# A recommendation network on one core: 32 table rows fetched by ScalarE's queue behind each part, three gathers fewer on GpSimd, logits laid out as 16 rows

## Chip, core and metric

One core of a Trainium2 chip runs the whole program. The metric is the device time of one execution in microseconds (us); lower is better. PE is the matrix engine (TensorE), ACT is ScalarE, DVE is VectorE, POOL is GpSimd and SP is SyncE, which here only issues DMAs.

## What is computed

A batch of 2048 samples, each with 13 dense numbers and 26 table indices, goes through this network (weights as arguments, batch norm over the batch):

```python
x = dense_inputs                                   # (2048, 13)
for W, b, g, be in bot:                            # 13 -> 512 -> 256 -> 64
    x = _bn(jax.nn.relu(x @ W + b), g, be)
embs = tbl[idx] for each of 26 tables              # (2048, 26, 64), tables of 12500 rows of 64 floats
T = concatenate([embs, x[:, None, :]], axis=1)     # (2048, 27, 64)
Z = einsum('bnd,bmd->bnm', T, T)
R = concatenate([x, Z[:, iu, ju]], axis=1)         # 64 + 351 columns
h = R
for W, b, g, be in top:                            # 415 -> 512 -> 256 -> 1
    h = _bn(jax.nn.relu(h @ W + b), g, be)
return sigmoid(h)
```

## The kernel before

Each engine runs a program of its own, written out by hand and tied to the others by semaphores only; there is no scheduler.

First comes the bottom network on the whole batch (to about 85 us). Meanwhile POOL has already begun to fetch table rows. The batch is cut into 16 parts of 128 samples (`PARTS`). A part needs 26 columns of embeddings, which stand as 13 pairs. One POOL gather (`indirect_dma_start`) fetches one of them for 128 partitions: 128 rows of 256 bytes. Embeddings lie in three slots (`emb[:, s]`), part i in slot i mod 3. POOL may begin a part when DVE has written its row numbers into `stage` (`slot_open`), which DVE does for part i+3 after it has copied part i out of its transposes.

Parts 0 to 14 go through a loop of 5 rounds by 3 slots (`LOOPS`, `SLOTS`). For each part:

- PE transposes the embeddings in four groups of pairs (group 3 is pair 12 alone, and waits for `landed[s][3]`), and DVE copies each group into `TT`. ACT has put the dense column `x` into `TT` (the activations from `x_all`).
- PE forms the products of all pairs, `z`, in two halves (banks `z_bank0` and `z_bank1`), then runs seven matmuls that serve nothing but to keep it busy (`keep_clock(7)`).
- ACT and DVE each copy half of `z` to `Zs` (`take_z`; ACT's half is 16 activations). PE waits for both (`z_taken_a`, `z_taken_v`) and then runs layer 0 of the top network for this part, four blocks of 16 matmul instructions.
- ACT applies Relu to each block twice (to `h0_part` and to `hidden0_hi`), DVE takes statistics.

The last part (15) goes through code of its own in halves h = 0 and 1, each with its own landing semaphores. Then follow layers 1 and 2 of the top network, the statistics of the logits, the sigmoid and one store.

SP shares in the fetch. Where POOL would need one gather, SP can issue 128 direct DMAs of one row each: it loads 16 row numbers into registers, then issues 16 DMAs, and so on. Before the change SP does this for one column of each part in slot 2 (five sets of 128), and for two columns of the last part (two sets of 128, in pieces), which land in a tile of their own, `emb_sp`. These 7 x 128 = 896 DMAs take the place of 7 gathers, so POOL issues 16 x 26 - 7 = 409.

ACT's loop body before, cut:

```python
with act.Fori(0, LOOPS) as it:
    for s in range(SLOTS):
        ...  # TT <- x_all, two activations (L693)
        for h in range(2):
            act.wait_ge(z_done, i * 2 + (h + 1))
            take_z(act_copy, z_bank[h], h, (2, 3)).then_inc(z_taken_a, 1)
        ...  # four blocks: L703, L705
```

Of the kernel before, what the change touches and what calls it, by code (L numbers as in the profile page):

```python
# [72 lines left out]
SP_SLOT = SLOTS - 1
SP_PAIR = TP - 1
SP_LAST = 2
SP_SETS = LOOPS + SP_LAST
SP_BATCH = 16
SP_ORDER = (("part", 0, 0, 128),
            ("last", 0, 0, 96),
            ("part", 1, 0, 128),  # L80
            ("last", 0, 96, 128),
            ("part", 2, 0, 128),
            ("last", 1, 0, 64),
            ("part", 3, 0, 128),
            ("last", 1, 64, 128),
            ("part", 4, 0, 128))
# [10 lines left out]
NPARAM = sum(w for _, w in PARAMS.values())  # L97
# [11 lines left out]
def rec_program(nc, idx, sp_idx, table, dense_t, params, identity, bw0, bw1, bw2, tw0x, twx, tw1, out):  # L109
    ctx = ExitStack()  # L110
    with ctx:
# [17 lines left out]
        sp_raw = sb("sp_raw", [SP_SETS, 2, P], I32)  # L129
        sp_neg = sb("sp_neg", [SP_SETS, P])  # L130
        sp_clamped = sb("sp_clamped", [SP_SETS, P])
        sp_rows = sb("sp_rows", [SP_SETS, P], U32)
        emb_sp = sb("emb_sp", [P, SP_LAST, D])
# [36 lines left out]
        tw2_rep = sb("tw2_rep", [P, K1, QUAD])  # L170
# [31 lines left out]
        consts_ready = sem("consts_ready")  # L202
        slot_open = sem("slot_open")
# [5 lines left out]
        landed_sp_part = sem("landed_sp_part")  # L209
        landed_sp_last = [sem("landed_sp_last%d" % k) for k in range(SP_LAST)]  # L210
# [96 lines left out]

        block = ctx.enter_context(nc.Block())


        @block.sync
        def _(sp):

            sp.dma_start(idx_raw[:, FIRST_COLS], idx[:, FIRST_COLS]).then_inc(first_idx_loaded, 16)
            sp.dma_start(idx_raw[:, LATER_COLS], idx[:, LATER_COLS]).then_inc(idx_loaded, 16)
            sp.dma_start(dense_sb[:, :], dense_t).then_inc(bottom_loaded, 16)
            sp.dma_start(sp_raw[:, :, :], sp_idx).then_inc(sp_idx_loaded, 16)
            sp.dma_start(bw0_sb[:, :], bw0).then_inc(bottom_loaded, 16)
# [10 lines left out]
            regs = [sp.alloc_register("sp_row%d" % r) for r in range(SP_BATCH)]  # L329
            sp.wait_ge(sp_rows_ready, 1)  # L330
            for kind, n, p0, p1 in SP_ORDER:
                if kind == "part":
                    sp.wait_ge(slot_open, n * SLOTS + SP_SLOT + 1)
                for at in range(p0, p1, SP_BATCH):
                    row_set = n if kind == "part" else LOOPS + n
                    sp.load(regs, sp_rows[row_set:row_set + 1, at:at + SP_BATCH])
                    for p, reg in enumerate(regs, at):
                        row = sp.snap(reg, min_val=0, max_val=NF * VOCAB - 1)
                        if kind == "part":
                            sp.dma_start(emb[p:p + 1, SP_SLOT, SP_PAIR, 0, :],  # L340
                                         table[bass.ds(row, 1), :]).then_inc(landed_sp_part, 16)
                        else:
                            sp.dma_start(emb_sp[p:p + 1, n, :],
                                         table[bass.ds(row, 1), :]).then_inc(landed_sp_last[n], 16)
# [49 lines left out]
        def _(pe):  # L394
# [85 lines left out]
            with pe.Fori(0, LOOPS) as it:  # L480
                for s in range(SLOTS):
                    i = it * SLOTS + s

                    for g in range(GROUPS):
                        pairs = group_pairs(g)
                        by_sp = 1 if s == SP_SLOT and SP_PAIR in pairs else 0
                        pe.wait_ge(landed[s][g], (it + 1) * ((len(pairs) * 2 - by_sp) * 16))
                        if by_sp:
                            pe.wait_ge(landed_sp_part, (it + 1) * (P * 16))
# [36 lines left out]
            def last_transposes(h, g):  # L526
# [3 lines left out]
                by_sp = SP_LAST if (h, g) == (0, 0) else 0  # L530
                pe.wait_ge(landed_last[h][g], (k1 - k0 - by_sp) * 16)
                for k in range(by_sp):
                    pe.wait_ge(landed_sp_last[k], P * 16)
# [75 lines left out]
            for k in range(K1):  # L609
                for j in range(CHUNKS):  # L610
                    mm = nc.tensor.matmul(out_bank[0][QUAD * j:QUAD * (j + 1), :], tw2_rep[:, k, :],  # L611
                                          hidden1[:, k, j * CHUNK:(j + 1) * CHUNK],
                                          start=(k == 0), stop=(k == K1 - 1))
                    if (k, j) == (0, CHUNKS - 1):

                        pe.wait_ge(scaled_v["top", 1], 2)
                        pe.wait_ge(bias_ready["top", 0], 1)
                        for kb in range(K1):
                            fold = nc.tensor.matmul(small[:, 8:9], ones[:, :], shift_w2[:, kb:kb + 1],
                                                    start=(kb == 0), stop=(kb == K1 - 1))  # L620
                        fold.then_inc(fold_done["top", 1], 1)
# [12 lines left out]
        def _(act):  # L634
# [52 lines left out]
            with act.Fori(0, LOOPS) as it:  # L687
                for s in range(SLOTS):
                    i = it * SLOTS + s

                    for h in range(2):
                        half = slice(h * D, (h + 1) * D)
                        last = nc.scalar.activation(TT[half, 0, :, NF:V].rearrange("p b v -> p (b v)"),  # L693
                                                    x_all[half, bass.ds(i * (2 * UNIT) + h * UNIT, UNIT)],
                                                    ACT.Copy)
                    last.then_inc(tt_x_written, 1)
# [3 lines left out]
                    for o in range(K0):  # L700
# [6 lines left out]
                                             bias=p_col("top", "b", 0)[:, o:o + 1]).then_inc(l0_relu, 1)  # L707

# [38 lines left out]
            nc.scalar.activation(logits[:, :], out_bank[0], ACT.Relu, bias=bias2["top"][:, :],  # L747
# [14 lines left out]
        def _(dve):  # L762
# [119 lines left out]
            nc.vector.memset(mean_of[:, :], 1.0 / (QUAD * B)).then_inc(consts_ready, 1)  # L882
# [191 lines left out]
```

## Time and profile before

| | |
|---|---|
| median of 3 runs | 573.51 us (572.97 to 573.55) |
| the profiled execution | 573.65 us, span 571.8 us |
| mean granted PE clock | 0.763 of full |
| busy PE / DVE / ACT / POOL | 66% / 42% / 33% / 68% |

The span runs from the first to the last instruction; the 1.85 us between the span and the execution's time lie around it. "Busy" counts an engine's own instructions; issuing a DMA from SP or ACT is not counted, so an engine can be occupied with nothing shown as busy. In the rows, SPq and ACTq are the sequencers of those engines.

### The profile page before, as it was taken

Reading aid. Unit: us, or ns where it says so; the run is one execution under the profiler, and the core shown is the slowest. Engines: PE = TensorE matmul, PEld = TensorE weight load, DVE = VectorE, ACT = ScalarE, POOL = GpSimd, SP = SyncE. Lnnn points to the kernel's source line nnn. Section 1 sums busy time; section 2 is a strip of 40 time slices with the busy share of each in tenths; the row PEclk is TensorE's granted clock in tenths of the full one; section 3 lists DMA queues with packets and bytes.
Section 4 is the critical chain, followed back from the end, with each engine's and each line's share of the span. In section 5 each row is a group of like instructions: output and inputs, shape, how many; then the busy total and the mean of one; then the engine's idle time right before and its main releaser. Section 6 shows DMA issues by size and latency. Waiting matters only on the chain.

```text
span 571.8 us, 16640 instructions
## 1 busy us (share of the span) xinstructions
PE 374.6 (66%) x5806; PEld 281.1 (49%) x5827; DVE 238.8 (42%) x650; ACT 189.5 (33%) x509; POOL 388.8 (68%) x419
## 2 busy tenths in 40 slices
PE   5959768678687572755729181754738182777995
PEld 2328536566565462543517171553526172566682
DVE  5773354644445342424323242423324242455522
ACT  4752144434244141323214041322314041464223
POOL 5777777777777777777777777777777777770100
PEclk9999886896786877585857666585858567598999
DMA  8322122222212221222122121222212121220000
GB/s 240 62 29 28 28 27 31 30 26 31 30 29 30 27 31 29 31 27 30 27 28 30 28 31 26 30 27 29 31 29 29 26 30 26 30 28 7 2 0 2
DMA packets 17500, 18.49 MB, mean 32 GB/s; under 512 B 9302, under 2 KB 10589, under 8 KB 17278
## 3 DMA queue, kind: packets, MB, share of 16 engines
q0 software_dynamic: 13088, 13.43, 17.6%
q1 hardware_dynamic: 4330, 3.96, 2.3%
q8 instruction: 54, 0.88, 0.7%
q14 instruction: 28, 0.22, 0.1%
HBM read 17.35 MB, written 0.01 MB: 30 GB/s over the span
## 4 chain that ended last, share of the span: by engine, by line
POOL 55%; issue 19%; PE 18%; DVE 2%; ACT 2%; DMA 1%; SPq 0%; POOLq 0%; DVEq 0%; ACTq 0%
POOL emb L367 52%; PE l_bank L442 6%; PE l_bank L458 5%; POOL emb L380 3%; PE l_bank L448 3%; PE l_bank L472 2%; PE l_bank L564 1%; DMA emb<-table,stage 1%; ACT Zs L306 1%; PE z_bank L400 1%; DMA par<-params 1%; DVE TT L916 0%; PE l_bank L611 0%; PE l_bank L561 0%; PE tr_bank L536 0%
## 5 line engine op out<-in xcount | busy, mean ns | idle before, releaser
L367 POOL DMA_INDIRECT emb<-table,stage x385 | 363.9, 945 | 120.3 <-issue 117.1
L306 ACT ACTIVATE Zs<-z_bank 27x112 f32<-27x112 f32 (+3 forms) x272 | 92.1, 339 | 200.8 <-PE z_bank L507 179.5
L493 PE MATMUL tr_bank<-ident,emb 128*128 128x128 f32 x195 | 39.1, 330 | 125.8 <-DMA emb<-table,stage 105.5
L280 DVE COPY Zs<-z_bank 27x112 f32<-27x112 f32 (+3 forms) x272 | 88.6, 326 | 51.1 <-PE z_bank L507 43.6
L521 PE MATMUL l_bank<-Zs,tw_sb 128*128 128x128 f32 x840 | 107.2, 281 | 0.0
L521 PEld LDWEIGHTS l_bank<-Zs,tw_sb 128*128 128x128 f32 x840 | 103.1, 199 | 0.0
L916 DVE COPY TT<-tr_bank 128x512 f32<-128x512 f32 (+1 forms) x60 | 54.6, 975 | 97.3 <-PE tr_bank L493 96.8
L493 PEld LDWEIGHTS tr_bank<-ident,emb 128*128 128x128 f32 x195 | 25.9, 163 | 137.5 <-issue 104.0
L507 PE MATMUL z_bank<-TT 64*27 64x26 f32 x3840 | 63.5, 219 | 31.8 <-issue 18.4
L507 PEld LDWEIGHTS z_bank<-TT 64*27 64x27 f32 x3840 | 55.4, 134 | 42.1 <-issue 38.1
L927 DVE BATCH_NORM_STATS2 stats_t<-h_part 128x128 f32 x60 | 17.7, 294 | 112.7 <-ACT hidden_hi L705 110.1
L703 ACT ACTIVATE h_part<-l_bank,par 128x128 f32<-128x128 f32 x60 | 22.1, 368 | 93.2 <-PE l_bank L521 90.0
L400 PE MATMUL tr_bank<-idle_operand 128*128 128x512 bf16 x95 | 42.6, 614 | 5.7 <-issue 5.7
L458 PE MATMUL l_bank<-hidden,bw_sb 13*128 13x512 f32 x32 | 27.7, 1061 | 6.1 <-DMA par<-params 6.1
L442 PE MATMUL l_bank<-hidden_hi,w_hi 128*128 128x512 f32 x64 | 26.4, 413 | 6.7 <-DVE w_hi L824 6.7
L518 PE MATMUL l_bank<-x_all,twx_sb 128*128 x120 | 27.5, 314 | 4.3 <-ACT Zs L306 3.9
L518 PEld LDWEIGHTS l_bank<-x_all,twx_sb 128*128 128x128 f32 x120 | 20.1, 211 | 16.9 <-issue 16.9
L380 POOL DMA_INDIRECT emb<-table,stage x24 | 22.6, 943 | 7.3 <-issue 7.3
L442 PE MATMUL l_bank<-hidden_lo,w_hi 128*128 128x512 f32 x64 | 26.0, 406 | 0.0
L400 PEld LDWEIGHTS tr_bank<-idle_operand 128*128 128x128 bf16 x112 | 13.6, 136 | 22.8 <-issue 21.3
L705 ACT ACTIVATE hidden_hi<-l_bank,par 128x128 f32 x60 | 21.6, 360 | 0.0
L458 PEld LDWEIGHTS l_bank<-hidden,bw_sb 13*128 13x128 f32 x32 | 10.5, 330 | 21.7 <-issue 15.1
(130 smaller groups left out, 279.2 us busy)
## 6 DMA issues: line engine op xcount, KB each, us to landing
emb<-table SPq DMA_DIRECT2D x640, 0.2 KB
emb<-table,stage POOLq DMA_INDIRECT x409, 2.8
emb_sp<-table SPq DMA_DIRECT2D x256, 0.2 KB
tw_sb<-tw0x SPq DMA_DIRECT2D x1, 1792.0 KB
bw_sb<-bw SPq DMA_DIRECT2D x1, 512.0 KB, 3.8
tw_sb<-tw SPq DMA_DIRECT2D x1, 512.0 KB
twx_sb<-twx SPq DMA_DIRECT2D x1, 256.0 KB
idx_raw<-idx SPq DMA_DIRECT2D x1, 169.0 KB, 2.5
```

Of the source, the lines that this page charges most:

```text
L280: last = copy(dst, src[:, :, ZC * q:ZC * q + w])
L306: return nc.scalar.activation(dst, src, ACT.Copy)
L367: pool.indirect_dma_start(out=emb[:, s, k, h, :], out_offset=None, in_=table, in_offset=bass.IndirectOffsetOnAxis(ap=stage[:, s, col:col + ...
L380: pool.indirect_dma_start(out=emb_last[:, h, k, :], out_offset=None, in_=table, in_offset=bass.IndirectOffsetOnAxis(ap=stage[:, LAST_SLOT, ...
L400: nc.tensor.matmul(bank[:, :], idle_operand[:, 0:P], idle_operand[:, :], start=True, stop=True)
L442: nc.tensor.matmul(bank, w1_scaled["hi"][:, k, o * P:(o + 1) * P], hidden0[part][:, k, ch * CHUNK:(ch + 1) * CHUNK], start=(n == 0 and par ...
L458: nc.tensor.matmul(bank, bw0_sb[:, o * P:(o + 1) * P], dense_sb[:, ch * CHUNK:(ch + 1) * CHUNK], start=True, stop=True).then_inc(mm_done[" ...
L493: tr = nc.tensor.transpose(tr_bank[g % 2][:, c * P:(c + 1) * P], emb[:, s, k, :, :].rearrange("p h d -> p (h d)"), ident[:, :])
L507: mm = nc.tensor.matmul(bank[QUAD * j:QUAD * j + V, x * ZM:(x + 1) * ZM], one, one[:, 1:V], start=True, stop=True)
L518: nc.tensor.matmul(acc, twx_sb[:, cols], x_all[:, bass.ds(i * (2 * UNIT), 2 * UNIT)], start=True, stop=False)
L521: mm = nc.tensor.matmul(acc, tw0_sb[:, c, cols], Zs[:, c, :], start=False, stop=(c == ZC - 1))
L916: nc.vector.tensor_copy(TT[:, 0, :, n0:n0 + w].rearrange("p b n -> p n b"), tr_bank[g % 2][:, 0:w * UNIT].rearrange("p (n b) -> p n b", n= ...
```

## The change

ACT's loop over the parts is written out instead of looping. Behind each of the parts 1 to 12 ACT issues 32 direct row DMAs (two loads of 16 row numbers, then 16 DMAs each). The column of slot 2 is still fetched whole by SP. A column of slot 1 is now fetched in rows too: for part 1 by SP alone, for parts 4, 7, 10 and 13 rows 0 to 31 by SP and 96 rows by ACT, a third behind each of the three parts ahead of it. The two columns of the last part go back to POOL. So rows take the place of 10 gathers, and POOL issues 16 x 26 - 10 = 406. `write_x(i + 1)`, ACT's copy of the dense column for the next part, now stands before the row DMAs. The logits are computed as a bank of 128 columns with 16 rows in use, instead of 512 columns with 4, by 32 narrow matmuls in place of 8 wide ones.

```diff
+LB = CHUNK // P
+LROW = QUAD // LB
...
-SP_ORDER = (("part", 0, 0, 128),
...
+ROW_SLOTS = (1, 2)
+ROW_BATCH = 16
+SP_ROWS = 32
+ACT_ROWS = P - SP_ROWS
+SP_ORDER = ((1, 0, P), (2, 0, P), (1, 1, SP_ROWS), (2, 1, P), (1, 2, SP_ROWS), (2, 2, P),
+            (1, 3, SP_ROWS), (2, 3, P), (1, 4, SP_ROWS), (2, 4, P))
...
+        def fetch_rows(engine, regs, slot, n, p0, p1):
+
+            row_set = ROW_SLOTS.index(slot) * LOOPS + n
+            for at in range(p0, p1, ROW_BATCH):
+                engine.load(regs, sp_rows[row_set:row_set + 1, at:at + ROW_BATCH])
+                for p, reg in enumerate(regs, at):
+                    row = engine.snap(reg, min_val=0, max_val=NF * VOCAB - 1)
+                    engine.dma_start(emb[p:p + 1, slot, ROW_PAIR, 0, :],
+                                     table[bass.ds(row, 1), :]).then_inc(landed_rows[slot], 16)
...
+            for slot, n, p1 in SP_ORDER:
+                sp.wait_ge(slot_open, n * SLOTS + slot + 1)
+                fetch_rows(sp, sp_regs, slot, n, 0, p1)
...
-                            if (s, k, h) == (SP_SLOT, SP_PAIR, 0):
+                            if s in ROW_SLOTS and (k, h) == (ROW_PAIR, 0):
                                 continue
...
-                        if h == 0 and k < SP_LAST:
-                            continue
...
+                        by_row = 1 if s in ROW_SLOTS and ROW_PAIR in pairs else 0
+                        pe.wait_ge(landed[s][g], (it + 1) * ((len(pairs) * 2 - by_row) * 16))
+                        if by_row:
+                            pe.wait_ge(landed_rows[s], (it + 1) * (P * 16))
...
-            with act.Fori(0, LOOPS) as it:
+            write_x(0)
+            for it in range(LOOPS):
                 for s in range(SLOTS):
...
+                    if i + 1 < LAST:
+                        write_x(i + 1)
+                    if 1 <= i <= LAST - SLOTS:
+                        n, third = divmod(i - 1, SLOTS)
+                        first = SP_ROWS + third * (ACT_ROWS // SLOTS)
+                        act.wait_ge(sp_rows_ready, 1)
+                        act.wait_ge(slot_open, (n + 1) * SLOTS + 2)
+                        fetch_rows(act, act_regs, 1, n + 1, first, first + ACT_ROWS // SLOTS)
...
-            nc.scalar.activation(logits[:, :], out_bank[0], ACT.Relu, bias=bias2["top"][:, :],
+            nc.scalar.activation(logits[:, :], out_bank[0][:, 0:P], ACT.Relu, bias=bias2["top"][:, :],
                                  accum_out=logit_sum[:, :]).then_inc(logit_summed, 1)
...
-                    last = nc.vector.tensor_scalar(tw2_rep[:, k, :], ones[:, 0:QUAD],
+                    last = nc.vector.tensor_scalar(tw2_col[:, k, 0:LB * QUAD:QUAD + LROW], ones[:, 0:LB],
```

Smaller edits that go with it: `tw2_col` is cleared at the start in place of filling `mean_of`, `mean_of` is then made from `ones` and a new column of `params` that is 1/2048 on every eighth partition, and the store writes 16 rows of 512 bytes instead of 4 of 2048.

On ACT, between the last Relu of one part and the first copy of `z` of the next, these instructions stand before the change (ISA and REGISTER_ALU are work on registers):

```order
L703 ACTIVATE h_part<-l_bank,par 128x128 [waits l0_done]
L705 ISA
L705 ACTIVATE hidden_hi<-l_bank,par 128x128
L693 ISA
L693 ACTIVATE TT<-x_all 64x64
L693 ISA
L693 ACTIVATE TT<-x_all 64x64
L698 ISA
L306 ACTIVATE Zs<-z_bank 27x16x7 [waits z_done]
```

After the change, at the same place between part 1 and part 2 (the middle of the 32 DMAs cut):

```order
L699 ACTIVATE h_part<-l_bank,par 128x128 [waits l0_done]
L701 ACTIVATE hidden_hi<-l_bank,par 128x128
L683 ACTIVATE TT<-x_all 64x64 x2
L307 TENSOR_LOAD sp_rows [waits slot_open,sp_rows_ready]
L309 ISA
L310 DMA emb<-table 1x64
...
L307 TENSOR_LOAD sp_rows
L309 ISA
L310 DMA emb<-table 1x64
...
L301 ACTIVATE Zs<-z_bank 27x16x7 [waits z_done]
```

Two loads and 32 pairs of a register instruction and a DMA now stand ahead of the first copy of the next part's `z`.

On POOL, the loop body and the last part before (x25 means 25 alike in a row):

```order
L367 DMA emb<-table,stage 128x64 [waits slot_open]
L367 DMA emb<-table,stage 128x64 x25
L360 REGISTER_ALU
L367 DMA emb<-table,stage 128x64 [waits slot_open]
L367 DMA emb<-table,stage 128x64 x25
L360 REGISTER_ALU
L367 DMA emb<-table,stage 128x64 [waits slot_open]
L367 DMA emb<-table,stage 128x64 x24
...
L380 DMA emb<-table,stage 128x64 [waits slot_open]
L380 DMA emb<-table,stage 128x64 x23
```

and after:

```order
L361 DMA emb<-table,stage 128x64 [waits slot_open]
L361 DMA emb<-table,stage 128x64 x25
L354 REGISTER_ALU
L361 DMA emb<-table,stage 128x64 [waits slot_open]
L361 DMA emb<-table,stage 128x64 x24
L354 REGISTER_ALU
L361 DMA emb<-table,stage 128x64 [waits slot_open]
L361 DMA emb<-table,stage 128x64 x24
...
L372 DMA emb<-table,stage 128x64 [waits slot_open]
L372 DMA emb<-table,stage 128x64 x25
```

Each round of three parts has one gather less, and the last part has two more.

## Rows read from the trace of the kernel before

**Rows 1.** Page: chain that ended last, by engine and line

```profile
POOL 55%; issue 19%; PE 18%; DVE 2%; ACT 2%; DMA 1%; SPq 0%; POOLq 0%; DVEq 0%; ACTq 0%
```

**Rows 2.** Timeline of POOL: start, length, operation, [idle before]; first and last gathers

```profile
4.48 1.13 POOL L367 DMA_INDIRECT emb<-table,stage  x1 [3.21 <-DVE stage L859]
5.92 0.94 POOL L367 DMA_INDIRECT emb<-table,stage  x1 [0.31 <-issue]
...
484.57 0.94 POOL L367 DMA_INDIRECT emb<-table,stage  x1 [0.30 <-issue]
...
508.28 0.94 POOL L380 DMA_INDIRECT emb<-table,stage  x1 [0.30 <-issue]
...
514.52 0.94 POOL L380 DMA_INDIRECT emb<-table,stage  x1 [0.30 <-issue]
```

**Rows 3.** Timeline from part 14 into the last part, all engines

```profile
487.55 0.47 PE L493 MATMUL tr_bank<-ident,emb 128*128 128x128 f32 x1 [0.24 <-DMA emb<-table,stage]
488.89 2.03 PE L507 MATMUL z_bank<-TT 64*27 64x26 f32 x132 [0.87 <-DVE TT L916]
...
491.11 2.88 ACT L306 ACTIVATE Zs<-z_bank 27x112 f32<-27x112 f32 x8 [15.71 <-PE z_bank L507]
...
505.21 0.27 PE L536 MATMUL tr_bank<-ident,emb_sp 128*128 128x128 f32 x1
...
509.69 4.27 ACT L306 ACTIVATE Zs<-z_bank 27x56 f32<-27x56 f32 x16 [1.60 <-PE z_bank L550]
...
512.55 1.11 PE L536 MATMUL tr_bank<-ident,emb 128*128 128x128 f32 x4 [2.07 <-DMA emb<-table,stage]
...
514.45 0.70 PE L561 MATMUL l_bank<-twx_sb,x_all 128*64 128x128 f32 x4
```

**Rows 4.** Timeline of ACT, parts 1 and 2 (start, length)

```profile
109.94 5.90 ACT L306 ACTIVATE Zs<-z_bank 27x112 f32<-27x112 f32 x16 [5.95 <-PE z_bank L507]
118.17 0.37 ACT L703 ACTIVATE h_part<-l_bank,par 128x128 f32<-128x128 f32 x1 [2.33 <-PE l_bank L521]
...
123.80 0.36 ACT L705 ACTIVATE hidden_hi<-l_bank,par 128x128 f32 x1
124.05 0.65 ACT L693 ACTIVATE TT<-x_all 64x64 f32 x2
130.59 2.89 ACT L306 ACTIVATE Zs<-z_bank 27x112 f32<-27x112 f32 x8 [5.89 <-PE z_bank L507]
```

**Rows 5.** Timeline of SP's queue: runs of DMA issues (start, length)

```profile
8.65 63.78 SPq L340 DMA_DIRECT2D emb<-table  x128
73.87 46.90 SPq L343 DMA_DIRECT2D emb_sp<-table  x96
...
194.23 14.76 SPq L343 DMA_DIRECT2D emb_sp<-table  x32
210.42 63.15 SPq L340 DMA_DIRECT2D emb<-table  x128
```

**Rows 6.** Lines of SP's queue: durations in ns min/median/max, first and last start

```profile
L336 SPq TENSOR_LOAD <-sp_rows x56: 1136/1229/1384, 7.2 to 459.8; - x56
L340 SPq DMA_DIRECT2D emb<-table x640: 224/225/567, 8.7 to 467.5; - x160
```

**Rows 7.** Register work on ACT's queue: durations in ns, first and last start

```profile
L705 ACTq FUSED_REGOPS  x45: 46/51/51, 99.3 to 505.4; - x45
```

**Rows 8.** Timeline of PE, layer 0 of parts 2 and 14

```profile
134.96 2.77 PE L400 MATMUL tr_bank<-idle_operand 128*128 128x512 bf16 x6 [0.33 <-issue]
138.04 0.79 PE L518 MATMUL l_bank<-x_all,twx_sb 128*128 x2 [0.31 <-ACT Zs L306]
138.62 2.38 PE L521 MATMUL l_bank<-Zs,tw_sb 128*128 128x128 f32 x14
140.84 0.39 PE L518 MATMUL l_bank<-x_all,twx_sb 128*128 x2
...
476.17 0.66 PE L493 MATMUL tr_bank<-ident,emb 128*128 128x128 f32 x4 [1.54 <-DMA emb<-table,stage]
486.19 1.11 PE L493 MATMUL tr_bank<-ident,emb 128*128 128x128 f32 x4 [9.36 <-DMA emb<-table,stage]
...
499.85 0.39 PE L518 MATMUL l_bank<-x_all,twx_sb 128*128 x2
501.64 0.39 PE L518 MATMUL l_bank<-x_all,twx_sb 128*128 x2
```

**Rows 9.** Windows: stretch, length, busy of PE, PEld, DVE, ACT, POOL, clock, DMA share, GB/s

```profile
467.00:478.00 11.00, 8.29 (x70) 7.81 (x68) 4.25 (x10) 3.03 (x10) 8.46 (x9) 0.97 0.22 26
478.00:498.00 20.00, 8.79 (x269) 5.77 (x271) 6.84 (x20) 5.61 (x16) 15.11 (x17) 0.50 0.20 28
498.00:512.00 14.00, 11.31 (x205) 9.95 (x205) 6.03 (x20) 6.73 (x21) 10.38 (x11) 0.99 0.22 29
```

**Rows 10.** Timeline of the end: logits, their statistics, sigmoid

```profile
563.33 1.06 PE L611 MATMUL l_bank<-hidden,tw_rep 128*32 128x512 f32 x8
564.46 0.69 ACT L747 ACTIVATE logits<-l_bank,bias_top 128x512 f32<-128x512 f32 x1 [4.19 <-PE l_bank L611]
565.97 0.72 ACT L751 ACTIVATE logit_sq<-logits,neg_mean 128x512 f32<-128x512 f32 x1 [0.73 <-DVE neg_mean L1011]
568.85 0.81 ACT L756 ACTIVATE prob<-logits,norm_top 128x512 f32<-128x512 f32 x1
```

More of the change, by code:

```diff
@@ L70 @@
 CHUNKS = B // CHUNK
+LB = CHUNK // P
+LROW = QUAD // LB
 CU = CHUNK // UNIT
 PW = NF
[L73 to L77, printed above, removed]
-SP_ORDER = (("part", 0, 0, 128),
[L79 to L86, printed above, removed]
+ROW_PAIR = TP - 1
+ROW_SLOTS = (1, 2)
+ROW_SETS = len(ROW_SLOTS) * LOOPS
+ROW_BATCH = 16
[3 more added lines that the diff above has]
+            (1, 3, SP_ROWS), (2, 3, P), (1, 4, SP_ROWS), (2, 4, P))
 FIRST_COLS = slice(0, SLOTS * PW)
@@ L96 @@
 PARAMS["top", "W", 2] = (sum(w for _, w in PARAMS.values()), K1)
-NPARAM = sum(w for _, w in PARAMS.values())
+NPARAM = sum(w for _, w in PARAMS.values()) + 1
 def group_pairs(g):
@@ L128, in rec_program @@
         stage = sb("stage", [P, SLOTS, PW], U32)
[L129 to L133, printed above, removed]
+        sp_raw = sb("sp_raw", [ROW_SETS, 2, P], I32)
+        sp_neg = sb("sp_neg", [ROW_SETS, P])
+        sp_clamped = sb("sp_clamped", [ROW_SETS, P])
+        sp_rows = sb("sp_rows", [ROW_SETS, P], U32)
         emb = sb("emb", [P, SLOTS, TP, 2, D])
@@ L174, in rec_program @@
         mean_of = sb("mean_of", [P, P])
-        logits = sb("logits", [P, CHUNK])
+        logits = sb("logits", [P, P])
         logit_sum = sb("logit_sum", [P, 1])
         neg_mean = sb("neg_mean", [P, 1])
-        logit_sq = sb("logit_sq", [P, CHUNK])
+        logit_sq = sb("logit_sq", [P, P])
         sq_sum = sb("sq_sum", [P, 1])
-        prob = sb("prob", [P, CHUNK])
+        prob = sb("prob", [P, P])
         tr_bank = [ps("tr_bank%d" % k, [P, GROUP * P]) for k in range(2)]
@@ L202, in rec_program @@
         consts_ready = sem("consts_ready")
+        mean_of_ready = sem("mean_of_ready")
         slot_open = sem("slot_open")
@@ L208, in rec_program @@
         sp_rows_ready = sem("sp_rows_ready")
-        landed_sp_part = sem("landed_sp_part")
-        landed_sp_last = [sem("landed_sp_last%d" % k) for k in range(SP_LAST)]
+        landed_rows = {s: sem("landed_rows%d" % s) for s in ROW_SLOTS}
         landed_last = [[sem("landed_last%d_%d" % (h, g)) for g in range(len(LAST_GROUPS))] for h in range(2)]
@@ L327, in _ @@
             sp.dma_start(w1_sb["top"][:, :, :], tw1.rearrange("(k p) n -> p k n", p=P)).then_inc(top_loaded, 16)
-            regs = [sp.alloc_register("sp_row%d" % r) for r in range(SP_BATCH)]
+            sp_regs = [sp.alloc_register("sp_row%d" % r) for r in range(ROW_BATCH)]
             sp.wait_ge(sp_rows_ready, 1)
[L331 to L344, printed above, removed]
+            for slot, n, p1 in SP_ORDER:
+                sp.wait_ge(slot_open, n * SLOTS + slot + 1)
+                fetch_rows(sp, sp_regs, slot, n, 0, p1)
             sp.wait_ge(prob_ready, 1)
-            sp.dma_start(out, prob[0:P:QUAD, :]).then_inc(stored, 16)
+            sp.dma_start(out.rearrange("q (j b) -> (q j) b", j=LB), prob[0:P:LROW, :]).then_inc(stored, 16)
             sp.wait_ge(stored, 16)
@@ L485, in _ @@
                         pairs = group_pairs(g)
[L486 to L489, printed above, removed]
+                        by_row = 1 if s in ROW_SLOTS and ROW_PAIR in pairs else 0
+                        pe.wait_ge(landed[s][g], (it + 1) * ((len(pairs) * 2 - by_row) * 16))
+                        if by_row:
+                            pe.wait_ge(landed_rows[s], (it + 1) * (P * 16))
                         if g >= 2:
@@ L529, in last_transposes @@
                 k0, k1 = LAST_GROUPS[g]
[L530 to L533, printed above, removed]
+                pe.wait_ge(landed_last[h][g], (k1 - k0) * 16)
                 for c, (k, k_end) in enumerate(last_blocks(g)):
-                    source = emb_sp if h == 0 and k < SP_LAST else emb_last[:, h, :, :]
                     tr = nc.tensor.transpose(last_tr_bank[g][0:(k_end - k) * D, c * P:(c + 1) * P],
-                                             source[:, k:k_end, :].rearrange("p k d -> p (k d)"),
+                                             emb_last[:, h, k:k_end, :].rearrange("p k d -> p (k d)"),
                                              ident[:, :])
@@ L609, in _ @@
             for k in range(K1):
[L610 to L621, printed above, removed]
+                for j in range(LB):
+                    for q in range(NQ):
+                        first = (q * LB + j) * P
+                        mm = nc.tensor.matmul(out_bank[0][QUAD * q:QUAD * (q + 1), 0:P],
+                                              tw2_col[:, k, j * QUAD:(j + 1) * QUAD], hidden1[:, k, first:first + P],
+                                              start=(k == 0 and j == 0), stop=(k == K1 - 1 and j == LB - 1))
+                if k == 0:
+                    pe.wait_ge(scaled_v["top", 1], 2)
+                    pe.wait_ge(bias_ready["top", 0], 1)
+                    for kb in range(K1):
+                        fold = nc.tensor.matmul(small[:, 8:9], ones[:, :], shift_w2[:, kb:kb + 1],
+                                                start=(kb == 0), stop=(kb == K1 - 1))
+                    fold.then_inc(fold_done["top", 1], 1)
             mm.then_inc(logits_done, 1)
             keep_clock(3, z_bank[0])
+            pe.wait_ge(mean_of_ready, 1)
             pe.wait_ge(logit_summed, 1)
@@ L686, in _, with write_x @@
             act.wait_ge(cleared, 1)
-            with act.Fori(0, LOOPS) as it:
+            act_regs = [act.alloc_register("act_row%d" % r) for r in range(ROW_BATCH)]
+            def write_x(i):
+                for h in range(2):
+                    half = slice(h * D, (h + 1) * D)
+                    last = nc.scalar.activation(TT[half, 0, :, NF:V].rearrange("p b v -> p (b v)"),
+                                                x_all[half, i * (2 * UNIT) + h * UNIT:i * (2 * UNIT) + (h + 1) * UNIT],
+                                                ACT.Copy)
+                last.then_inc(tt_x_written, 1)
+            write_x(0)
+            for it in range(LOOPS):
                 for s in range(SLOTS):
                     i = it * SLOTS + s
[L691 to L696, printed above, removed]
                     for h in range(2):
@@ L881, in _ @@
             nc.vector.memset(eps_col[:, :], EPS).then_inc(consts_ready, 1)
-            nc.vector.memset(mean_of[:, :], 1.0 / (QUAD * B)).then_inc(consts_ready, 1)
+            nc.vector.memset(tw2_col[:, :, :], 0.0).then_inc(consts_ready, 1)
             dve.wait_ge(consts_ready, 5)
             dve.wait_ge(bottom_loaded, 48)
+            nc.vector.tensor_scalar_mul(mean_of[:, :], ones[:, :], par[:, NPARAM - 1:NPARAM]).then_inc(mean_of_ready, 1)
             for n in range(CHUNKS * K0):
@@ L1044 @@
         params[:, at:at + width] = columns(vec)
+    params[0:P:LROW, NPARAM - 1] = 1.0 / B
     w0 = get("L0_rec_top_W0")
@@ L1054 @@
     cols = idx.reshape(UNIT * 2, PARTS, TP, 2)
-    sets = ([(it * SLOTS + SP_SLOT, SP_PAIR) for it in range(LOOPS)] + [(LAST, k) for k in range(SP_LAST)])
+    sets = [(it * SLOTS + s, ROW_PAIR) for s in ROW_SLOTS for it in range(LOOPS)]
     sp_idx = np.stack([np.stack([cols[:, part, k, 0], (2 * k + np.arange(P) // UNIT) * VOCAB]) for part, k in sets])
```

2 lines of the change are left out of this document (1 added, 1 removed).

## The prediction

> **What bounds the kernel now.** I read the chain that ended last first: POOL has 55% of it and "issue" 19%, most of it the pause between POOL's gathers [rows 1]. POOL's timeline shows why: from 5.92 to 484.57 us gathers 2 to 385 start every 1.25 us (478.65 / 383) and POOL never waits for anything, neither for a slot nor for a transfer [rows 2]. So each gather is worth 1.25 us until the last part. There, [rows 3] show that other bounds stand close: part 14's chain gives PE back at 505.2; the last part's copies of `z` end at 509.69 + 4.27 = 513.96; the gather begun at 508.28 [rows 2] lets PE transpose at 512.55; and both meet at the layer 0 that starts at 514.45. The end goes by whichever is later: POOL, or the chain over PE and ACT.
>
> The second view is therefore ACT's timeline. Between parts it looks free: before part 14 it waits 15.71 us for `z` [rows 3]. But in parts 1 and 2 it waits only 5.9 us [rows 4], since PE has only just begun on the parts (the bottom network ran until 85 us) and catches up with POOL: a part takes 130.59 - 109.94 = 20.65 us there, against some 32 in POOL's pace.
>
> **POOL's term.** Three gathers fewer by 1.25 us: -3.75 us, if POOL still sets the end. `slot_open` gives POOL a lead of two whole parts, some 63 us, so a part that is up to that much late doesn't stop it.
>
> **What a fetch costs ACT.** The trace has no DMA issued by ACT. The nearest rows are SP's, which runs the same load, register instruction and DMA in the same order. 32 rows with one load among them took 14.76 us [rows 5], and the load ahead adds about 1.3 (the gap from 72.43 to 73.87), so 16.0 us. From below: were all but the DMAs' own 225 ns and the loads' shortest 1136 ns hidden [rows 6], 32 x 0.225 + 2 x 1.14 = 9.5 us. Nothing at all is excluded, since the DMAs stand in the same queue ahead of the next copy of `z`. From above: with each DMA as long as the longest of SP's, 567 ns instead of 225 [rows 6], 16.0 + 32 x 0.34 = 26.9 us. I take 16.0: register work costs ACT's queue 51 ns [rows 7], small as on SP, and SP's pace is the only measured one for this whole sequence.
>
> The DMA engines aren't the issue: they are busy 0.20 to 0.22 of the time [rows 9], and 384 rows of 256 bytes on ACT are in number what 3 gathers fetch.
>
> **ACT's period with the fetch.** From the first copy of `z` to the end of `TT<-x_all` ACT takes 124.70 - 109.94 = 14.8 us [rows 4]. All of this waits on itself: PE's layer 0 needs ACT's copies, the Relus need layer 0. With 16.0 behind it the period is 30.8 us. That fits into POOL's 31.7 (76 gathers for three parts, 95.0 us) by a hair. But two things don't fit.
>
> First, the last third of the rows for parts 4, 7, 10 and 13 is issued directly ahead of that very part. PE can finish its transposes only when they have landed: from a gather's end at 485.51 to PE's transpose 2.0 us, to `z` 1.4, to ACT's copy 2.2, in sum 5.6 us [rows 2, 3] in which ACT waits. Three parts then take ACT 3 x 30.8 + 5.6 = 98.0 us, more than POOL's 95.0.
>
> Second, the catching up is gone. Before, parts went at 20.65 us until PE reached POOL at about part 5. Now they go at 30.8 from part 1 on and never reach it.
>
> **The chain, step by step.** Copies of `z` of part 1 start at 109.94, as before. SP must issue 256 rows for parts 1 and 2 instead of 128: 73.87 + 63.4 = 137.3 [rows 5], plus 5.6, so part 2's copies start at 142.9 (ACT itself is free at 140.7; before it was 130.59). Part 3: 173.7. Part 4: 173.7 + 30.8 + 5.6 = 210.1. Part 13: 210.1 + 3 x 98.0 = 504.1. Behind it stands no fetch, so part 14 follows at the quick pace: 524.8. Before it was 491.11 [rows 3]. All that follows stands on this: **+33.7 us**, and POOL's 3.75 are hidden below it. The last part's rows have all landed by then; its own chain over copies and layer 0 is as long as before, so 0 here. SP's later sets stay ahead of need: part 5's end at 137.3 + 16.0 + 65 = 218, and PE could use them at about 228.
>
> **PE's clock.** PE now idles ahead of layer 0. In a period of 30.8 us it has the same work of about 20.65, so about 10 us of nothing between the last filler matmul and layer 0, in the seven parts (3, 5, 6, 8, 9, 11, 12) where ACT isn't waiting for rows. In the trace an idle of 9.36 us [rows 8] was followed by a granted clock of 0.50, which is 1.2 GHz, for the 20 us from 478 to 498, after 0.97 ahead of it [rows 9]. A block of layer 0 takes 1.79 us at 2.4 GHz (499.85 to 501.64) and up to twice that at 1.2; part 2's first block, caught on the rise, took 2.80 [rows 8]. I take one block at half clock in each of the seven: 7 x 1.8 = **+12.5 us**. The bounds are 0, and all four blocks slow, 7 x 7.2 = +50. The Trainium skill ("TensorE: Matmul & The Clock Gate", HAM oscillation) says that a wait for data lets the clock drop, so that the next batch starts cold each time; by that rule the term is at least mine. The trace agrees for the waits on gathers, and shows none yet for a wait on ACT.
>
> **Logits.** Three activations shrink from 512 to 128 columns: 0.69, 0.72 and 0.81 us [rows 10] become about 0.37, as the 128-column Relu in [rows 4] does, so -1.1. PE's half on the path, 8 instructions in 1.06 us [rows 10], becomes 32 of a quarter of the width: the same columns, with more instructions, 0 to +0.8; I take +0.3. Together **-0.8**. The multiply for `mean_of` and the larger clear fall where DVE waits for PE in the bottom network; uncovered they would be some 0.5 us. The unrolling takes a few register instructions from ACT, hidden in its waits before.
>
> **Sum.** 573.65 (the profiled execution's own time, 0.14 above the median) + 33.7 + 12.5 - 0.8 = 619.1, forecast **619 us**.
>
> **Rivals.** (1) *ACT issues faster than SP, and the change does what POOL's row promises.* ACT's lateness falls by 12 us for each us by which a fetch is shorter (12 fetches in the chain). To be back at part 14's new due time, 491.1 - 3.75, it must lose 37.4 us, so the fetch must take 12.9 us or less. Then POOL sets the end: 573.65 - 3.75 - 0.8 = 569.1 us, faster. For it: the lower bound 9.5 is inside; ACT's long wait in steady state [rows 3] is as long as one fetch. Against it: 225 ns are only half of SP's measured step of 0.42 us, and I see no reason for the other half to vanish on ACT. The skill's page "Perfetto Trace Analysis" (DMA Optimizations) would have it so: where descriptor generation binds, balancing DMAs over the engines that can issue them may help. By that rule the result would be 569. Its page "DMA: Bandwidth & Descriptors" (Issuing engines are not separate DMA queues) says that this saves only the issuing sequencer's time; no run here shows either yet. Chance 0.18.
>
> (2) *The fetch is as on SP, but the clock stays low through layer 0* (or the fetch is slower by 2 us): 573.65 + 33.7 + 50 - 0.8 = 657 at the full bound; 643 with 18 us a fetch and my clock term. Above 650: chance 0.10.
>
> (3) *The fetch lies between*, 13 us, and the loss cancels the gain within 0.2% (what a measurement of this kernel can just tell from no change, 1.1 us): only a window of 0.2 us in the fetch's length does this. Chance 0.02.
>
> (4) *The forecast*: fetch of 14 to 18 us, some clock loss. From 573.65 + 33.7 - 24 - 0.8 = 583 (14 us, no clock loss) to 619 + 24 = 643 (18 us), with a longer clock loss 650. Chance 0.70; its own range is 583 to 650. Above 0.2% slower in all: 0.80, rival 2 within it. The range over all reaches from rival 1's 568 to 650.
>
> **What the profile after should show.** Runs of 32 row DMAs in ACT's queue of 16 us each (if about 12, rival 1). Gathers still 1.25 us apart, the last starting at about 510.8, with PE going on long after. ACT's first copies of `z` about 31 us apart in two of three parts and 36 in the third, waiting for no one in the two. Part 13's copies near 504 plus the clock's share. PE idle 10 us ahead of layer 0, with the clock at 0.5 there. The forecast is wrong if ACT still waits for `z` in most parts, or if the rows' landing isn't what PE waits for in parts 4, 7, 10 and 13.

## The result and the profile after

The changed kernel takes 602.93 us (median of 4, 601.71 to 603.51) against 573.52 us before: a ratio of 1.0497, with a 95% interval of 1.0471 to 1.0524. It is slower by 29.4 us. The profiled execution took 603.06 us with a span of 601.2 us. Here and below a ratio leaves out executions that lie more than 1.5% above the fastest of their kernel.

The page of the profile of the kernel after, the chain that ended last by engine and by line, answers to [rows 1]:

```profile
PE 46%; ACTq 23%; ACT 15%; issue 10%; DVE 4%; DMA 1%; SPq 0%; DVEq 0%
PE l_bank L513 19%; ACTq L310 16%; ACT Zs L301 12%; PE l_bank L434 5%; PE l_bank L450 5%; PE z_bank L499 4%; ACTq L307 4%; PE l_bank L510 4%; ACTq L309 3%; PE l_bank L440 3%; PE l_bank L464 2%; DVE TT L921 2%; PE l_bank L552 1%; ACT TT L683 1%; DMA emb<-table 1%
```

POOL had 55% of the chain before; now it isn't in it. In its place stands ACT's queue (ACTq) with 23%: L310 issues the row DMAs, L307 loads row numbers, L309 is the register instruction. POOL itself did just what the prediction's term for it says. Its last gather, the 406th, against 514.52 before [rows 2]:

```profile
511.04 1.04 POOL L372 DMA_INDIRECT emb<-table,stage  x1 [0.31 <-issue]
```

It starts 3.5 us sooner, and PE goes on with parts long after. ACT's waits, sums over the span (us in total, times, longest):

```profile
ACT Zs L301 <- issue: 114.5, 8, 14.5
ACT h_part L699 <- PE l_bank L513: 112.0, 60, 4.2
ACT Zs L301 <- PE z_bank L499: 92.9, 11, 19.3
```

In 8 parts ACT comes to its copies of `z` with no wait for PE: the idle time of its datapath, up to 14.5 us each, ends by "issue", which is the queue at work on DMAs. The timeline of ACT shows a period (parts 3, 4 and 5; start, length, engine, operation, idle before):

```profile
173.03 5.66 ACT L301 ACTIVATE Zs<-z_bank 27x112 f32<-27x112 f32 x16 [14.37 <-issue]
...
189.42 0.36 ACT L701 ACTIVATE hidden_hi<-l_bank,par 128x128 fp32r<-128x128 f32 x1
189.67 0.66 ACT L683 ACTIVATE TT<-x_all 64x64 f32<-64x64 f32 x2
190.57 14.00 ACTq L310 DMA_DIRECT2D emb<-table  x32
209.66 2.89 ACT L301 ACTIVATE Zs<-z_bank 27x112 f32<-27x112 f32 x8 [19.33 <-PE z_bank L499]
...
223.70 0.36 ACT L701 ACTIVATE hidden_hi<-l_bank,par 128x128 fp32r<-128x128 f32 x1
223.95 0.66 ACT L683 ACTIVATE TT<-x_all 64x64 f32<-64x64 f32 x2
224.86 14.23 ACTq L310 DMA_DIRECT2D emb<-table  x32
239.14 3.20 ACT L301 ACTIVATE Zs<-z_bank 27x112 f32<-27x112 f32 x9 [14.53 <-issue]
```

The reader is to see two things. From 224.86 to 239.09 the queue issues, and the copies of part 5 start at 239.14, at once. From 190.57 to 204.57 it issues the last third for part 4, and then ACT waits 5.1 us more, until 209.66: rows landing, transpose, `z`. Later copies start at 499.38 (part 13) and 519.86 (part 14), against 459.43 and 491.11 before: part 14 is 28.8 us late, and that is nearly the whole loss of 29.4.

Most of this lateness is there early. Part 4's copies start at 209.66 against 175.78 before, and from part 4 to part 13 ACT takes 96.6 us for each round of three parts (289.72 / 3), only 1.6 us more than POOL's 95.0. Part 14, with no fetch ahead of it, then wins some back.

The queues' rows, durations in ns min/median/max, answer to [rows 6]:

```profile
L310 ACTq DMA_DIRECT2D emb<-table x384: 213/214/524, 129.5 to 494.6; - x192
L307 ACTq TENSOR_LOAD <-sp_rows x24: 1184/1249/1537, 128.1 to 487.3; - x24
```

PE's timeline in part 5, from the end of its filler on, answers to [rows 8]:

```profile
234.00 2.52 PE L392 MATMUL tr_bank<-idle_operand 128*128 128x512 bf16 x6 [0.33 <-issue]
245.05 0.79 PE L510 MATMUL l_bank<-x_all,twx_sb 128*128 x2 [8.53 <-ACT Zs L301]
245.63 3.19 PE L513 MATMUL l_bank<-Zs,tw_sb 128*128 128x128 f32 x14
248.62 0.64 PE L510 MATMUL l_bank<-x_all,twx_sb 128*128 x2
249.05 2.01 PE L513 MATMUL l_bank<-Zs,tw_sb 128*128 128x128 f32 x14
250.89 0.39 PE L510 MATMUL l_bank<-x_all,twx_sb 128*128 x2
```

and the windows over it (the granted clock is the third number from the right):

```profile
239.00:250.00 11.00, 4.95 (x24) 4.96 (x25) 0.36 (x2) 6.10 (x18) 8.30 (x9) 0.53 0.25 29
250.00:262.00 12.00, 7.72 (x123) 6.69 (x121) 5.03 (x12) 2.41 (x8) 9.22 (x10) 1.00 0.20 31
```

After 8.53 us without work the first block of layer 0 takes 3.57 us (245.05 to 248.62), twice the 1.79 of [rows 8], in a window with 0.53 granted (near the lower level, 1.2 GHz); the second takes 2.27, and from 250 on the clock is 1.00 (2.4 GHz). In all seven parts where PE waits for ACT (3, 5, 6, 8, 9, 11, 12) the first block takes 3.57 us, the second 2.12 to 3.05, and the third 1.79.

### The profile page after: what moved, and what is told of

Its sections match the earlier page's. It is cut to its first block, busy times and chain, and to the rows that moved or that the text cites. A ratio compares the mean times of both kernels' runs of the same rounds, so it can differ in the third digit from the quotient of the medians.

```text
span 601.2 us, 17737 instructions
## 1 busy us (share of the span) xinstructions
PE 390.2 (65%) x5853; PEld 300.9 (50%) x5875; DVE 236.4 (39%) x651; ACT 187.4 (31%) x509; POOL 386.3 (64%) x416
## 4 chain that ended last, share of the span: by engine, by line
PE 46%; ACTq 23%; ACT 15%; issue 10%; DVE 4%; DMA 1%; SPq 0%; DVEq 0%
PE l_bank L513 19%; ACTq L310 16%; ACT Zs L301 12%; PE l_bank L434 5%; PE l_bank L450 5%; PE z_bank L499 4%; ACTq L307 4%; PE l_bank L510 4%; ACTq L309 3%; PE l_bank L440 3%; PE l_bank L464 2%; DVE TT L921 2%; PE l_bank L552 1%; ACT TT L683 1%; DMA emb<-table 1%
## 5 line engine op out<-in xcount | busy, mean ns | idle before, releaser
L513 PE MATMUL l_bank<-Zs,tw_sb 128*128 128x128 f32 x840 | 123.7, 308 | 0.0
L513 PEld LDWEIGHTS l_bank<-Zs,tw_sb 128*128 128x128 f32 x840 | 119.8, 226 | 0.0
L485 PE MATMUL tr_bank<-ident,emb 128*128 128x128 f32 x195 | 33.8, 305 | 94.6 <-DMA emb<-table 61.5
L499 PE MATMUL z_bank<-TT 64*27 64x26 f32 x3840 | 66.1, 217 | 30.0 <-issue 14.2
L921 DVE COPY TT<-tr_bank 128x512 f32<-128x512 f32 (+1 forms) x60 | 52.4, 980 | 64.1 <-PE tr_bank L485 63.7
L485 PEld LDWEIGHTS tr_bank<-ident,emb 128*128 128x128 f32 x195 | 23.8, 151 | 103.4 <-issue 71.7
L510 PE MATMUL l_bank<-x_all,twx_sb 128*128 x120 | 30.4, 343 | 51.3 <-ACT Zs L301 51.3
L510 PEld LDWEIGHTS l_bank<-x_all,twx_sb 128*128 128x128 f32 x120 | 22.9, 237 | 63.4 <-issue 63.4
L701 ACT ACTIVATE hidden_hi<-l_bank,par 128x128 fp32r<-128x128 f32 x60 | 21.6, 360 | 0.0
```

Of the source, the lines that this page charges most:

```text
L485: tr = nc.tensor.transpose(tr_bank[g % 2][:, c * P:(c + 1) * P], emb[:, s, k, :, :].rearrange("p h d -> p (h d)"), ident[:, :])
L499: mm = nc.tensor.matmul(bank[QUAD * j:QUAD * j + V, x * ZM:(x + 1) * ZM], one, one[:, 1:V], start=True, stop=True)
L510: nc.tensor.matmul(acc, twx_sb[:, cols], x_all[:, bass.ds(i * (2 * UNIT), 2 * UNIT)], start=True, stop=False)
L513: mm = nc.tensor.matmul(acc, tw0_sb[:, c, cols], Zs[:, c, :], start=False, stop=(c == ZC - 1))
L921: nc.vector.tensor_copy(TT[:, 0, :, n0:n0 + w].rearrange("p b n -> p n b"), tr_bank[g % 2][:, 0:w * UNIT].rearrange("p (n b) -> p n b", n= ...
```

## The experiments

In each, "stretch" is the time from ACT's first copy of a part's `z` to the end of its last Relu. The kernels with 28 and 24 rows, with rows set aside and with more filler ran once each, so their times have no interval; the differences read from their times are 12 us and more, where the executions of the kernel before lie within 5 us (572.88 to 577.59). More filler, at 3 us, is read by its trace.

**ACT issues no rows.** The changed kernel without ACT's fetches; 96 of 128 rows of one column stay unfetched in parts 4, 7, 10 and 13.

```diff
-                    if 1 <= i <= LAST - SLOTS:
...
-                        fetch_rows(act, act_regs, 1, n + 1, first, first + ACT_ROWS // SLOTS)
...
-                            pe.wait_ge(landed_rows[s], (it + 1) * (P * 16))
+                            pe.wait_ge(landed_rows[s], (it + 1) * (P * 16) if s != 1 else P * 16 + it * ((SP_ROWS + 3 * ACT_FETCH) * 16))
```

> The changed kernel, but ACT issues no row DMAs: 96 of the 128 rows of one column in parts 4, 7, 10 and 13 are not fetched, and PE waits for SP's 32 alone. Theory (ACT's fetch sets the pace): PE catches up with POOL again by about part 5, POOL's 406 gathers set the end, 573.65 - 3.75 - 0.8 = about 569 us. Rival (it is SP's 256 rows for parts 1 and 2, or the unrolled ACT program, that cost the time): still above 585.

Measured: 568.24 us (567.42 to 569.04), a ratio to before of 0.9876 (0.9831 to 0.9922). ACT's timeline at part 14:

```profile
485.36 2.87 ACT L302 ACTIVATE Zs<-z_bank 27x112 f32<-27x112 f32 x8 [15.39 <-PE z_bank L500]
```

ACT waits for PE again, and part 14 is 5.8 us ahead of before. SP's rows for part 2 are still late there (its copies start at 141.75 against 130.59), and it costs nothing at the end. The 34.7 us between this kernel and the changed one are ACT's fetches, with the wait for their rows and the clock that they cost, and without them the gathers saved bring the kernel to about the 569.1 us of the prediction's first rival.

**28 and 24 rows in each fetch.** The second load and its DMAs cut short, the rest of the rows not fetched.

```diff
-                        fetch_rows(act, act_regs, 1, n + 1, first, first + ACT_ROWS // SLOTS)
+                        fetch_rows(act, act_regs, 1, n + 1, first, first + ACT_FETCH)
```

> The changed kernel with 28 rows in each of ACT's 12 fetches instead of 32 (4 rows in each third are not fetched). Theory: each fetch is 4 x 0.38 to 0.40 = 1.6 us shorter and all 12 lie on the chain, so 602.9 - 19 = about 584 us. Rival (lateness comes once, from the start, not from each fetch): within 3 us of the changed kernel.

> As the kernel with 28, with 24 rows in each fetch. The chain over ACT would come to 602.9 - 38 = 565 us, below POOL's bound of 569; so 569 to 573 by the theory, bent by the floor and not 38 below. Rival (one-time lateness): no change from 602.

Measured: 585.88 and 568.92 us. From 32 to 28 rows the time falls by 17.1 us, 1.4 for each of 12 fetches; from 28 to 24 by another 17.0, down to about the kernel with no rows on ACT. Part 5's copies stand at 239.14, 232.57 and 227.38 us with 32, 28 and 24, part 13's at 499.38, 479.92 and 458.99. The steps grow from 6.6 and 5.2 us to 19.5 and 20.9, so the lateness comes with each fetch and not once. With 28 rows the fetch behind part 1 isn't on the chain: part 2 waits for SP's rows, until 143.36. And with 24 ACT waits 11.49 us for `z` ahead of part 14, against 6.06 with 28, so by then it has some 5 us to spare and is out of the bound.

One thing more stands in these two traces. A round of three parts, from part 4's copies to part 13's, takes 91.7 us with 28 rows and 86.1 with 24. With 28 ACT is thus quicker than POOL's 95.0, and the kernel is still 12.4 us slower than before: it reaches part 4 late (204.90 against 175.78) and hasn't caught up by part 14.

**Rows set aside.** ACT issues all 384 DMAs, into a tile that nobody reads; PE doesn't wait for them, so 96 rows of the column are old ones.

```diff
+                        engine.dma_start(aside[p:p + 1, aside_at, :],
+                                         table[bass.ds(row, 1), :]).then_inc(landed_aside, 16)
```

> The changed kernel with ACT's 384 rows landing in a tile that no one reads until the end; PE waits for SP's 32 rows alone in parts 4, 7, 10 and 13 (96 rows of that column are not the right ones). It takes away the wait for rows just issued and keeps ACT's queue as it is. Theory: the four waits of 5.1 us go, and PE then idles ahead of layer 0 in those parts too, at some 2 us of slow clock each: 602.9 - 20 + 8 = about 590 us. Rival (landing of the rows is the whole trouble): 569.

Measured: 587.66 us. ACT's waits:

```profile
ACT Zs L304 <- issue: 156.7, 11, 14.4
ACT h_part L706 <- PE l_bank L520: 111.0, 60, 4.1
ACT Zs L304 <- PE z_bank L506: 35.3, 7, 18.6
```

"Issue" now ends the wait in 11 parts instead of 8, and of the 29.4 us lost 14 remain. So the wait for the landing of rows just issued costs about 15 us net, and the occupied queue alone, with no data needed, still puts the kernel above before.

**More filler.** 29 filler matmuls instead of 7 in slots 0 and 2.

```diff
-                    keep_clock(7, tr_bank[0])
+                    keep_clock(7 if s == 1 else 29, tr_bank[0])
```

> The changed kernel with 29 filler matmuls instead of 7 behind z in slots 0 and 2 (parts 0, 2, 3, 5, 6, 8, 9, 11, 12, 14). They fill 5 to 9 us of PE's wait for ACT. Theory (a low clock lengthens layer 0 behind that wait): in parts 3, 5, 6, 8, 9, 11 and 12 the stretch from ACT's first copy to its last Relu falls from 16.0-16.9 to about 14.3 us, 15 us in all, while parts 0 and 14, where ACT doesn't make PE wait, pay up to 5 us each: 588 to 598 us. Rival (the longer stretch has another cause, such as contention with the row DMAs): the stretches stay above 16 us.

Measured: 599.96 us, 2 us above the expected range. PE's timeline in part 5, and in part 8:

```profile
235.48 5.75 PE L392 MATMUL tr_bank<-idle_operand 128*128 128x512 bf16 x24
244.52 0.48 PE L510 MATMUL l_bank<-x_all,twx_sb 128*128 x2 [3.29 <-ACT Zs L301]
244.84 1.73 PE L513 MATMUL l_bank<-Zs,tw_sb 128*128 128x128 f32 x14
246.41 0.39 PE L510 MATMUL l_bank<-x_all,twx_sb 128*128 x2
...
328.71 7.78 PE L392 MATMUL tr_bank<-idle_operand 128*128 128x512 bf16 x28 [0.34 <-issue]
339.35 0.79 PE L510 MATMUL l_bank<-x_all,twx_sb 128*128 x2 [2.87 <-ACT Zs L301]
339.94 3.19 PE L513 MATMUL l_bank<-Zs,tw_sb 128*128 128x128 f32 x14
342.92 0.64 PE L510 MATMUL l_bank<-x_all,twx_sb 128*128 x2
```

In part 5, with 3.29 us idle instead of 8.53, the first block takes 1.89 us. In parts 3, 5 and 9 the stretch fell from 16.1-16.8 to 14.0 us, as expected; in 6, 11 and 12 only to 15.5-15.7, and in part 8 not at all (16.9). Over the seven parts it went from 115.3 to 105.9 us, 9.4 of the 15 I had expected. Part 14 paid: its layer 0 starts 4.6 us after its copies are done.

So the slow blocks hang on what PE does ahead of them: nothing but filler was added, and in three parts they went. But the length of the idle time just ahead of layer 0 doesn't sort the parts. In 3, 5 and 9 it was 1.64, 3.29 and 1.42 us, and the first block took 1.88 or 1.89. In 6, 8, 11 and 12 it was 1.85, 2.87, 2.65 and 2.12 us, no longer than in part 5, and the first block took 3.14 to 3.57; part 8's ran at 0.50 granted. What set the clock in those four stays open. As a cure, filler is a poor one.

**Logits alone,** put on the kernel before (the diff's parts on `tw2_col`, `mean_of`, `logits` and `prob`).

```diff
-            nc.scalar.activation(logits[:, :], out_bank[0], ACT.Relu, bias=bias2["top"][:, :],
+            nc.scalar.activation(logits[:, :], out_bank[0][:, 0:P], ACT.Relu, bias=bias2["top"][:, :],
```

> The kernel before with the logits' new layout alone. By the prediction's term 0.8 us less than before, 0.9 by the stretch from the scaled weights to the end in the trace after (9.66 against 10.56 us): 572.6 us. Rival (the 64 narrow matmul instructions or the extra work at the start eat it): 573.5 or more.

Measured: 572.64 us, ratio 0.9964 (0.9946 to 0.9981): 1.1 to 3.1 us less, clear of no change. Its timeline at the end, against [rows 10]:

```profile
563.39 1.08 PE L616 MATMUL l_bank<-hidden,tw_col 128*32 128x128 f32 x32
564.53 0.37 ACT L753 ACTIVATE logits<-l_bank,bias_top 128x128 f32<-128x128 f32 x1 [4.20 <-PE l_bank L616]
...
565.78 0.40 ACT L757 ACTIVATE logit_sq<-logits,neg_mean 128x128 f32<-128x128 f32 x1 [0.79 <-DVE neg_mean L1018]
...
568.34 0.49 ACT L762 ACTIVATE prob<-logits,norm_top 128x128 f32<-128x128 f32 x1
```

The activations took 0.96 us less in sum, and PE's half 1.08 us against 1.06: the narrow matmuls cost next to nothing. The whole time's interval begins just above the 0.8 us forecast; the size of the gain rests on these rows.

**Rows late.** ACT fetches only once PE has caught up: behind parts 4 to 12, and 32 rows of the last part behind part 13; POOL gathers the column in parts 1 and 4. Nothing is left out.

```diff
+                    if 3 * FROM - 2 <= i <= LAST - SLOTS:
...
+                    if i == LAST - 2:
+                        fetch_rows(act, act_regs, "last", 1, 96, 128)
```

> A version meant to keep the gain: ACT fetches rows only once PE has caught up with POOL, behind parts 4 to 12 (for parts 7, 10 and 13) and 32 rows of the last part behind part 13; POOL gathers the column itself in parts 1 and 4; SP keeps its two columns of the last part less those 32 rows; 406 gathers, new logits. Theory: from part 5 on ACT's idle time of 15.7 us holds the fetch's 15, POOL sets the end: 569 to 571 us. Rival (ACT's queue has no room even there, because the rows for the next part hold PE up by 5 us each loop and the clock falls): 575 to 585.

Measured: 578.87 us, the median of 12 runs that lie far apart (570.9 to 583.61). The theory's 569 to 571 is missed, and the rival's 575 to 585 holds it. The ratio is 1.0032 (0.9999 to 1.0065), and only from the 8 runs up to 579.29; the other 4 lie at 579.93 to 583.61, and the median of all is 0.8% above that of before. So there is no gain, and whether there is a small loss isn't told. ACT's timeline of the profiled execution (578.56 us):

```profile
465.60 2.89 ACT L306 ACTIVATE Zs<-z_bank 27x112 f32<-27x112 f32 x8 [19.82 <-PE z_bank L514]
469.26 2.87 ACT L306 ACTIVATE Zs<-z_bank 27x112 f32<-27x112 f32 x8 [0.77 <-PE z_bank L514]
481.90 14.09 ACTq L316 DMA_DIRECT2D emb_sp<-table  x32
496.03 4.25 ACT L306 ACTIVATE Zs<-z_bank 27x112 f32<-27x112 f32 x12 [14.34 <-issue]
```

Part 13 starts 6 us later than before; ACT's queue was done at 460.07, and 5.5 us went by until the rows had landed and `z` was there. The fetch behind it takes away the pause in which ACT could have made that good: part 14 starts 5 us later than before. Against the changed kernel part 5 starts 32.4 us earlier (206.79) and part 13 33.8 us earlier: all of the distance is there by part 5. So the lost catching up was most of the 29 us (here it is kept, and by the medians 24 of them are gone), and a fetch of 32 has no room in steady state either.

**24 rows, complete,** with nothing left out: ACT 24 rows in each fetch, SP 56 of that column and all of slot 2's, POOL the column in part 1; 407 gathers. One version loads 16 and 8 row numbers, the other all 24 at once.

```diff
-SP_ROWS = 32
+SP_ROWS = 56
...
+SP_ORDER = ((2, 0, 0, P), (1, 1, 0, SP_ROWS), (2, 1, 0, P), (1, 2, 0, SP_ROWS), (2, 2, 0, P),
+            (1, 3, 0, SP_ROWS), (2, 3, 0, P), (1, 4, 0, SP_ROWS), (2, 4, 0, P))
```

> A complete kernel cut to what the runs so far allow: ACT fetches 24 rows behind each of parts 1 to 12 in place of 32, SP 56 of the column in parts 4, 7, 10 and 13 and the whole column in slot 2; POOL gathers the column itself in part 1, and the last part's two; 407 gathers, new logits. The kernel with 24 rows that left rows out came to 568.9. Theory: ACT's period of some 29 us plus the wait for rows stays within POOL's 31.7, one gather more costs 1.25: 570 to 571 us, 0.5% under before. Rival (SP, which now has 184 rows per round, 93 us of 95, is late with part 14's rows and sets the end): 573 to 576.

> As the complete kernel with 24 rows, but ACT loads all 24 row numbers at once instead of 16 and 8. The second load's 1.2 us goes from each of the 12 fetches. Theory: if ACT's chain still touches the end, up to 1.5 us less than with two loads; if POOL alone sets it, the same within 0.3 us, 570 to 571 us. Rival (a load's time grows with the number of registers, so nothing is saved on ACT): same as with two loads in the fetch's length too.

Measured: 570.09 and 569.75 us, both with a ratio to before of 0.9924 (0.9900 to 0.9947 and 0.9902 to 0.9947). Both take 0.8% less than the kernel before, a small gain that is clear of the interval. The version with one load, ACT at part 14:

```profile
488.00 2.89 ACT L306 ACTIVATE Zs<-z_bank 27x112 f32<-27x112 f32 x8 [16.13 <-PE z_bank L514]
```

ACT waits for PE, and part 14 is 3.1 us ahead of before. Between the two versions no difference can be told.

## Why the prediction was right

The time forecast was 619 us, 16 above the measured one: of the loss of 45 us forecast, 29 came. The direction, the bound and the chain were right; the sizes were off both ways.

**The bound and POOL's term.** Right: gathers 1.25 us apart, never stopped, hidden under ACT's lateness. That three fewer are worth having was shown by the kernel without ACT's rows.

**ACT's period.** The mechanism was right in each step, its main size 1.85 us too long. I had 14.8 + 16.0 = 30.8 us. Measured from the last Relu to the next copies: 14.5 to 15.1 us in the parts where ACT doesn't wait. Over all 11 fetches from part 2 on, less the four waits for rows, that is 14.75 us on average, on a stretch of 14.2 at full clock, together about 28.95. Two reasons. ACT's queue steps from DMA to DMA in 0.377 us (median) where SP's takes 0.416. And the load of row numbers begins before the last Relu has ended (at 189.22 in part 3, the Relu ends at 189.78), so that it and `TT<-x_all` lie beside each other, where the sum had them one behind the other. Over the 11 fetches from part 2 on this makes 20 us. Part 14 came 17.4 us earlier than forecast (519.86 against 524.8 + 12.5 = 537.3): 20 by the period and 3 by shorter waits for rows, less what the slow clock took beyond its term. Behind that start another 1.5 us were lost, most of them in part 14's own stretch (16.25 us against 14.93 before).

**The wait for rows.** 5.6 us forecast, 5.1, 4.9, 4.7 and 4.5 measured. Setting the rows aside showed that it is a cause of its own. With it a round of three parts takes 96.6 us, above POOL's 95.0 as forecast (98.0).

**The catching up.** Right in that it was lost, and its early numbers are close in part by luck: part 2's copies at 143.6 (forecast 142.9), part 3's at 173.0 (173.7), part 4's at 209.7 (210.1). The forecast had part 2 wait for SP's rows. In fact ACT's own queue held it until 143.54, since part 1 began 2.2 us later than before and its stretch was 16.5 us. Part 3's slow stretch (16.75) then hid most of the shorter period; from part 4 on it shows.

**The clock.** Forecast +12.5 us in seven parts; measured 115.3 - 7 x 14.2 = 15.9 in those, and some 4 more in parts 1, 2 and 7. The size of the first block was right (3.57 against 1.79 in each of the seven); the second block is slow in part (2.12 to 3.05), which I had left out. Rival 2's full bound of 50 us never came near: the clock was back at 1.00 by the second or third block. The rule cited from the Trainium skill ("TensorE: Matmul & The Clock Gate", HAM oscillation), that a wait for data lets the clock drop and the next batch starts cold, agrees with these seven waits, now on ACT. How long the idle time must be isn't shown: see more filler.

**Logits.** Forecast -0.8, measured 572.82 - 573.65 = -0.8 between profiled executions. By the ratio it is 1.1 to 3.1 us, so the exact agreement of two single executions is partly luck; the rows bear the 0.96 us of the activations.

**The rivals.** Rival 1's condition was a fetch of 12.9 us or less. With 28 rows the queue is busy 13.3 to 13.9 us and the kernel is slow; with 24 it is busy 11.6 to 11.9 us, and the rival's 569.1 came out (568.92). Two numbers in the condition were off. In the loop five gathers are saved, not three (two come back in the last part), so at POOL's pace part 14 is due some 6 us earlier and not 3.75: at 485.36 in the kernel without ACT's rows. And the sum counts 12 fetches where its own chain has part 2 wait for SP, which leaves 11. The rule of the Trainium skill that balancing DMAs over the issuing engines may help ("Perfetto Trace Analysis", DMA Optimizations) agrees with the kernels with 24 rows (0.9924); with 32 the same step is a loss of 5%.

## What to carry to other kernels

An engine's mean idle time between its tasks is no room to fill. Ask what its period becomes with the added work in the stretch where the kernel catches up, what waits for the result of that work at once, and whether the other engine's clock survives the wait. A period that fits the slower engine's pace isn't yet enough, as the kernel with 28 rows shows: lateness from the start must be made good before the end. And when an added cost is repeated, vary its size in two steps and look at an early part and a late one: a difference that grows from part to part, down to a floor, shows both the cause and the size that is safe.

## What the hardware showed that I had not expected

The same sequence for one row DMA steps in 0.377 us on ACT and 0.416 on SP; the DMA itself is 214 and 225 ns. A load of registers grows with their number: 16 took 1.25 us and 24 took 1.67 on ACT, so one load of 24 shortened the fetch by some 0.6 us and not by the 1.2 of a whole load. Rows of the one-load version:

```profile
L313 SPq TENSOR_LOAD <-sp_rows x56: 782/1228/1376, 7.2 to 471.9; - x56
L313 ACTq TENSOR_LOAD <-sp_rows x12: 1666/1671/1694, 123.3 to 437.7; - x12
```

SP's shortest there, 782 ns, are loads of 8. Open stays why the runs of the kernel with late rows lie 13 us apart, while those of the others don't; this wasn't followed up.
